# Start addresses in SBUF: every tile that TensorE reads moved to a multiple of 64 bytes

## The chip, the cores and the metric

The kernel runs on one core of a Trainium2 chip. The metric is the time of one execution on the device in microseconds (us), as a median of several executions. A core has five engines: TensorE (PE) multiplies matrices, VectorE (DVE), ScalarE (ACT) and GpSimd (POOL) do elementwise work, and SyncE (SP) issues transfers. A matmul has two inputs, both read from SBUF, the memory of 128 partitions beside the engines: the stationary one (here mostly 128 columns), which is loaded ahead, and the moving one, whose columns (here mostly 512 or 272) then stream through. Each tile of SBUF begins at the same byte offset in every partition; that offset is what this case changes.

## The reference

The input is x (64 sequences of 32 tokens, 512 features). Two layers follow, each added to x:

```
x = x + lora_moe_0(long_convolution(x))      # W_base, 8 experts of rank 16, top 2
x = x + lora_moe_1(paged_attention(x))       # same form, other weights
long_convolution: a kernel of 512 taps per channel from a state space model, masked by length
paged_attention:  q = x Wq (32 heads of 128), k, v = x Wk, x Wv (8 heads), RMS norm and rotation
                  of q and k, 512 cached keys per sequence found by a block table plus 32 own
                  keys, softmax, times the values, times Wo
lora_moe:         x W_base + b + sum over experts of weight * (x A_e) B_e
```

All is float32. To keep its precision on the faster path (type fp32r), the kernel splits a factor into an upper and a lower part (names ending in `hi` and `lo`) and multiplies three times: hi by hi, hi by lo and lo by hi.

## The kernel before, in words

The program is one long sequence of stages, and each engine has its own list of instructions, written out by hand, with semaphores between them. There is no planner.

- `prologue`: turns the cached keys (L378), computes the taps, and convolves (L399).
- `ffn` for layer 0: gate (L625), base product (L666, L667, L671: 192 matmuls of 512 columns in 4 column blocks of 48), first factor of the experts (L648 to L650: 48 matmuls), second factor (L681 to L683: 48 matmuls). Moving are `xh`, `xl`; stationary are the halves of the weights, `pr_hi` and `pr_lo`. For the second factor moving is `f_hw`, stationary `f_lb`.
- `project`: 160 tiles of queries and keys, then 32 tiles of values. A tile is 12 matmuls of 512 columns (L762 hi*hi, L763 hi*lo, L764 lo*hi, four times), with `xh` or `xl` stationary and the weights moving. For queries and keys a tile also takes four transposes on PE (L981, five tiles later) and, on the other engines, squares (ACT L868), the mean (DVE L904), the root (ACT L880), the reciprocal (DVE L908), the normed tile `pr_qn` (DVE L911), the two products with the tables of the rotation (DVE L922, POOL L942, two instructions) and their sum (DVE L918). In four of 16 tiles DVE also makes the lower half of the next weights (L751). PE writes the tiles to four banks of PSUM in turn, and so waits for L911 of four tiles earlier. Values need none of this: ACT copies them out (L893) and SP stores them.
- `attention`: 512 steps, one head of one sequence each. A step has 6 matmuls of 272 columns for the scores (L1209), 4 transposes (L1218) and 4 matmuls with the cached values (L1242); every fourth step adds own values (L1249).
- `output_projection`: 32 units, 8 groups of heads by 4 blocks of 512 tokens. A unit is 48 matmuls of 512 columns: for each of 4 column blocks, 8 of L1529 and L1530 (upper and lower weights by `op_ohi`) and 4 of L1534 (upper weights by `op_olo`). Units alternate between two buffers of the moving operand: units 0, 2, ... read `op_ohi0` and `op_olo0`, units 1, 3, ... read `op_ohi1` and `op_olo1`. The stationary `op_whi` and `op_wlo` change every 4 units.
- `ffn` for layer 1: as for layer 0, with `f1_x_hi` and `f1_x_lo` moving and `f1_w_hi` and `f1_w_lo` stationary.

Tiles are placed one behind the other, each start rounded up to 32 bytes, from the left by `sbuf_tensor` and from the right with `side="right"`; `Early` and `Late` place tiles at offsets counted from `place`, the end of `shared`. The table of constants is 769 numbers wide, 3076 bytes, so `shared` and what stands behind it begin 32 bytes past a multiple of 64.

Of the kernel before, what the change touches and what calls it, by code (L numbers as in the profile page):

```python
# [15 lines left out]
F32 = mybir.dt.float32  # L16
# [7 lines left out]
P = 128  # L24
B, S, L = 64, 32, 512
T = B * S
KB = L // P
NS = 64
HP = S // 2
E, R = 8, 16  # L30
# [7 lines left out]
KC = LK // P  # L38
# [21 lines left out]
C_ROW = C_DESC + E  # L60
C_REV = C_ROW + KB
C_MOD = C_REV + KB
C_ALL = C_MOD + 1


def constants():

    c = np.zeros((P, C_ALL), np.float32)
    c[:, C_ID:C_ID + P] = np.eye(P)
# [13 lines left out]
class Line:  # L83


    def __init__(self, eng, sem):
        self.eng, self.sem, self.n = eng, sem, 0
# [54 lines left out]
def prologue(nc, ps, dram, taps, cst, um, mrow, k_t, y_t, cos, sin, ta, tb, inputs):  # L142
# [9 lines left out]
    with ExitStack() as ctx:  # L152
# [32 lines left out]
        with nc.Block() as block:  # L185
            @block.sync
            def _(e):
                src = bass.AP(tensor=dram["L0_cond_log_dt"].tensor, offset=0, ap=[[0, P], [1, S]])
                e.dma_start(log_dt[:, :], src).then_inc(s_dt, 16)
                e.dma_start(raw[:, 1, :], dram["log_a"]).then_inc(s_dt, 16)  # L190
                e.dma_start(ai[:, :], dram["a_imag"]).then_inc(s_in, 16)
                e.dma_start(cc[:, :, :], dram["c"]).then_inc(s_in, 16)
                e.dma_start(dvec[:, :], dram["L0_cond_D"].rearrange("(o h) -> o h", o=1)).then_inc(s_in, 16)

                def load(n):
                    e.dma_start(k_in[:, n % TB, :], dram["k_cache"][n * P:(n + 1) * P, :]).then_inc(s_ki[n % TB], 16)

                for n in range(TB):
                    load(n)
                k_rows = k_t.rearrange("(t n d) x -> t d n x", n=PPT, d=P)  # L200
                for n in range(KT):
                    e.wait_ge(s_kc, 2 * (n + 1))
                    e.dma_start(k_rows[n:n + 1, :, :, :].rearrange("o d n x -> (o d) n x"),
                                k_out[:, n % TB, :, :, :].rearrange("p n g k -> p n (g k)")).then_inc(s_ko[n % TB], 16)
                    if n + TB < KT:
                        load(n + TB)
                    if n + TB == KT:
                        inputs.load(e, dram, ("w0", "b0", "g0", "a0", "lb0"))
                for q in range(TB):
                    e.wait_ge(s_ko[q], 16 * KT // TB)  # L210
# [106 lines left out]
            def _(e):  # L317
# [39 lines left out]
                for h in range(TOE):  # L357
                    load(h)
# [48 lines left out]
class Inputs:  # L407


    def __init__(self, nc, ctx, sems, tag, at=None):  # L410
        def sb(n, shape):
            if at is None:
                return ctx.enter_context(nc.sbuf_tensor(f"f{tag}_{n}", shape, F32))
            x = nc.alloc_sbuf_tensor_at(f"f{tag}_{n}", shape, F32, offset=self.end)
            self.end += (math.prod(shape[1:]) * 4 + 31) // 32 * 32
            return x

        self.end = at
        self.w = sb("w", [P, KB, L])
        self.a = sb("a", [P, KB, E * R])  # L420
        self.g = sb("g", [P, KB, S])
        self.lb = sb("lb", [E * R, L])
        self.bias = sb("bias", [P, KB])
        self.s_z, self.s_g, self.s_w, self.s_a, self.s_b = (
            sems.enter_context(nc.semaphore(f"f{tag}_{n}")) for n in ("s_z", "s_g", "s_w", "s_a", "s_b"))

# [4 lines left out]
    def load(self, e, dram, names):  # L431

        w_n, b_n, g_n, a_n, lb_n = names
        e.wait_ge(self.s_z, 1)
        e.dma_start(self.g[:, :, 0:E], dram[g_n].rearrange("(k p) e -> p k e", p=P)).then_inc(self.s_g, 16)
        e.dma_start(self.w[:, :, :], dram[w_n].rearrange("(k p) o -> p k o", p=P)).then_inc(self.s_w, 16)
        e.dma_start(self.bias[:, :], dram[b_n]).then_inc(self.s_w, 16)
        e.dma_start(self.a[:, :, :], dram[a_n].rearrange("(k p) r -> p k r", p=P)).then_inc(self.s_a, 16)
        e.dma_start(self.lb[:, :], dram[lb_n]).then_inc(self.s_b, 16)

# [546 lines left out]
        return s_proj, s_stage, s_t, s_qr, stores  # L987


LATE_SMALL = 4 * (KB * (L + E * R + S) + L + KB)  # L990


class Early:
# [3 lines left out]
    def __init__(self, nc, sems, at):  # L997
        def place(n, shape, d=F32):
            size = math.prod(shape[1:]) * 4
            x = nc.alloc_sbuf_tensor_at("at_" + n, shape, d, offset=self.end)  # L1000
            self.end += (size + 31) // 32 * 32
            return x

        self.end = at
        self.v_raw = place("v_raw", [P, 2, KC, HK * D])
        self.leni = place("leni", [P, B], I32)
        self.lenf = place("lenf", [P, B])
        self.pagef = place("pagef", [P, B * KC])
        self.rows = place("rows", [P, B * KC], U32)
        self.page = place("page", [P, B * NPP], I32)  # L1010
        self.idx = place("idx", [P, 2, KC], U32)
        self.mask = place("mask", [P, 2, NKEY])
        self.pr_new = place("pr_new", [P, 2, REP * S])
        self.nm, self.su, self.ri = (place(n, [P, 2 * REP]) for n in ("nm", "su", "ri"))
        place("gap", [P, 168])
        self.q_hi = place("q_hi", [P, 2, HK * P], F32R)
        self.ot = place("ot", [P, 2, HK * P])

        self.chunks = [nc.alloc_sbuf_tensor_at(f"f0_resid{q}", [P, KB, 512], F32, offset=self.end - (1 - q) * 4 * 2 * 2 * HK * P)
                       for q in range(2)]  # L1020
        self.more = nc.alloc_sbuf_tensor_at("pr_more", [P, 2, 512], F32, offset=self.end + 4 * HK * P)
        self.q_lo = place("q_lo", [P, 2, HK * P], F32R)
        self.v_new = place("v_new", [P, 2, 2, REP * D])
        self.k_hi, self.k_lo = (place(n, [P, 2, 2, NKEY], F32R) for n in ("k_hi", "k_lo"))
        place("gap2", [P, 256])
        place("gap4", [P, 2 * LK])
        place("gap3", [P, 32])
        self.s_in, self.s_qhi = (sems.enter_context(nc.semaphore("at_" + n)) for n in ("in", "qhi"))
# [7 lines left out]
class Late:  # L1036
# [4 lines left out]
    def __init__(self, nc, sems, at, keys):  # L1041
        def place(n, shape, offset, d=F32):
            return nc.alloc_sbuf_tensor_at(n, shape, d, offset=offset)

        w, o = REP * L * 4, 512 // S * P * 4
        small = at + 2 * KC * HK * D * 4
        sums = small + (LATE_SMALL + 31) // 32 * 32
        split = sums + KB * T * 4
        self.w_hi, self.w_lo = ([place(f"op_w{h}{q}", [P, REP, L], at + (2 * q + i) * w, F32R) for q in range(2)]
                                for i, h in enumerate(("hi", "lo")))  # L1050
        self.o_hi, self.o_lo = ([place(f"op_o{h}{q}", [P, REP, 512], (keys + i * o, split + i * 2 * 2 * NKEY * 4)[q], F32R)
                                 for q in range(2)] for i, h in enumerate(("hi", "lo")))
        self.att = place("att", [P, KB, T], sums)
        self.x_hi = place("f1_x_hi", [P, KB, T], at, F32R)
        self.inputs = Inputs(nc, None, sems, "1", small)
        self.end = split
        self.s_whi, self.s_wlo, self.s_ohi, self.s_olo = (sems.enter_context(nc.semaphore("op_" + n)) for n in ("whi", "wlo", "ohi", "olo"))
# [482 lines left out]
def build(nc, dram, out_t):  # L1540
# [9 lines left out]
    with ExitStack() as ctx:  # L1550
        ps = ctx.enter_context(nc.psum_tensor("ps", [P, 8, 512], F32))
        cst = ctx.enter_context(nc.sbuf_tensor("constants", [P, C_ALL], F32))

        KT_SIZE, QK_SIZE = 2 * (NPP + 1) * HK * PSIZE, 2 * HK * P
        shared = ctx.enter_context(nc.sbuf_tensor("shared", [P, KT_SIZE + QK_SIZE], F32))
        y_t = shared[:, 0:KB * T].rearrange("p (k t) -> p k t", k=KB)
        angles = shared[:, KB * T:KB * T + NT * D].rearrange("p (two t h) -> p two t h", two=2, t=NT)
# [5 lines left out]
        place = nc.sbuf_base  # L1563
        with ExitStack() as sems:
            sb = lambda c, n, s, d=F32, side=None: c.enter_context(nc.sbuf_tensor(n, s, d, side=side))
# [80 lines left out]
```

## Time and profile before

| | us |
|---|---|
| median of 3 runs | 2441.7 (2440.74 to 2443.94) |
| the profiled execution, whole | 2454.87 |
| its span, first to last instruction | 2453.0 |
| PE busy in it | 2400.6 |
| DVE busy in it | 1878.4 |
| ACT busy in it | 1310.2 |
| POOL busy in it | 719.9 |

The profile is of one execution. Matmuls overlap, and the end of each is modelled, so the time that a matmul costs in a stream is the distance between two starts. The granted clock of TensorE is given as a share of full speed, which is 2.4 GHz; its mean here is 0.997.

### The profile page before, as it was taken

The page shows a single profiled execution, that of the slowest core. Times are in us where ns is not written, and L with a number is a line of the kernel's source. Part 1 is how long each engine was busy: PE and PEld are TensorE (multiplying, and loading weights), DVE is VectorE, ACT ScalarE, POOL GpSimd, SP SyncE. Part 2 cuts the span into 40 slices and gives each one's busy share as a digit, 9 for nine tenths or more (in the row PEclk, how much of TensorE's full clock was granted, in tenths as well). Part 3 has the DMA queues.
Part 4 walks back from the last instruction along what each step waited for, and adds up shares of the span by engine and source line. Part 5 has one row for each costly group of instructions (what it writes and reads, how often), then busy time and mean ns, then how long its engine had stood idle before and what let it go on. Part 6 is the DMA issues. An engine that isn't in the chain of part 4 may idle for free. (4 is left out here: it accounts for less than half of the span.)

```text
span 2453.0 us, 53992 instructions
## 1 busy us (share of the span) xinstructions
PE 2400.6 (98%) x16104; PEld 2167.1 (88%) x16104; DVE 1878.4 (77%) x3317; ACT 1310.2 (53%) x3758; POOL 719.9 (29%) x712
## 2 busy tenths in 40 slices
PE   5999999999999999999999999999999999999999
PEld 4888777777777999999999999999999998888877
DVE  7559999999961887788778877788778876666653
ACT  2335555555543677677767776676667761111120
POOL 1206666666641122222222222222222213131100
PEclk9999999999999999999999999999999999999999
DMA  8732333333347688888888888888788879666622
GB/s 312 258 120 87 94 98 95 95 115 94 98 125 245 222 295 276 294 298 291 281 285 303 295 284 282 293 297 295 273 295 295 295 268 283 219 209 207 204 69 103
DMA packets 434117, 542.36 MB, mean 221 GB/s; under 512 B 36980, under 2 KB 350100, under 8 KB 429460
## 3 DMA queue, kind: packets, MB, share of 16 engines
q1 hardware_dynamic: 390724, 394.24, 48.7%
q0 software_dynamic: 36864, 134.23, 16.2%
q10 hardware_dynamic: 6480, 13.26, 1.5%
q8 instruction: 28, 0.46, 0.1%
q14 instruction: 21, 0.17, 0.0%
HBM read 440.59 MB, written 101.01 MB: 221 GB/s over the span
## 5 line engine op out<-in xcount | busy, mean ns | idle before, releaser
L1296 DVE CUSTOM_DVE_ANT_0 at_sm<-ps,at_mask 128x544 f32<-128x544 f32 x512 | 369.3, 721 | 256.2 <-PE ps L1209 247.7
L1242 PE MATMUL ps<-at_pt,at_v_raw 128*128 128x128 f32 x4096 | 540.9, 275 | 1.7 <-issue 1.7
L1242 PEld LDWEIGHTS ps<-at_pt,at_v_raw 128*128 128x128 f32 x4096 | 497.6, 192 | 1.9 <-issue 1.9
L1359 ACT ACTIVATE at_pt<-ps 128x512 f32<-128x512 f32 x512 | 303.9, 594 | 299.4 <-PE ps L1218 194.9
L942 POOL TENSOR_TENSOR pr_m<-pr_qn,tb 128x256 f32<-128x256 f32 x320 | 331.6, 1056 | 307.0 <-DVE pr_qn L911 291.8
L1372 ACT ACTIVATE at_pr<-at_sm,at_nm 128x544 f32<-128x544 f32 x512 | 383.1, 748 | 59.1 <-DVE at_nm L1296 54.9
L1289 DVE TENSOR_TENSOR at_k_lo<-shared,at_k_hi 128x1088 fp32r<-128x1088 f32 x256 | 325.9, 1273 | 0.0
L762 PE MATMUL ps<-pr_hi,xh 128*128 (+1 forms) x768 | 317.7, 414 | 6.1 <-DVE pr_qn L911 5.0
L1167 POOL DMA_INDIRECT at_v_raw<-v_cache,at_idx x256 | 276.9, 1082 | 113.9 <-issue 62.0
L1218 PE MATMUL ps<-constants,at_pr 128*128 128x128 f32 x2048 | 306.5, 272 | 0.0
L764 PE MATMUL ps<-pr_hi,xl 128*128 (+1 forms) x768 | 303.3, 395 | 0.0
L763 PE MATMUL ps<-pr_lo,xh 128*128 (+1 forms) x768 | 303.2, 395 | 0.0
L868 ACT ACTIVATE pr_sq<-ps 128x128 f32<-128x128 f32 x640 | 168.0, 277 | 229.7 <-DVE f_a L904 224.4
L1173 POOL COPY at_idx<-at_rows 128x4 uint32 (+1 forms) x64 | 11.8, 184 | 868.4 <-PE ps L1249 801.7
L1209 PE MATMUL ps<-at_k_hi,at_q_hi 128*128 128x272 f32 x1024 | 255.5, 330 | 3.1 <-issue 1.2
L1218 PEld LDWEIGHTS ps<-constants,at_pr 128*128 128x128 f32 x2048 | 243.5, 140 | 0.0
L1209 PE MATMUL ps<-at_k_hi,at_q_lo 128*128 128x272 f32 x1024 | 211.9, 288 | 0.0
L1209 PE MATMUL ps<-at_k_lo,at_q_hi 128*128 128x272 f32 x1024 | 211.2, 287 | 0.0
L1477 ACT ACTIVATE op_ohi<-o_raw 128x2048 fp32r<-128x2048 f32 x31 | 59.6, 1922 | 273.5 <-PE ps L1534 243.1
L1530 PE MATMUL ps<-op_ohi,op_wlo 128*128 128x512 f32 x512 | 201.2, 393 | 0.0
L1529 PE MATMUL ps<-op_ohi,op_whi 128*128 128x512 f32 x512 | 200.9, 392 | 0.0
L922 DVE TENSOR_TENSOR pr_m<-pr_qn,ta 128x512 f32<-128x512 f32 x160 | 195.9, 1224 | 0.0
(239 smaller groups left out, 4299.3 us busy)
## 6 DMA issues: line engine op xcount, KB each, us to landing
shared<-k_t SPq DMA_DIRECT2D x1024, 128.0 KB
qk_t<-pr_stage SPq DMA_DIRECT2D x160, 256.0 KB, 2.3
shared<-qk_t SPq DMA_DIRECT2D x64, 512.0 KB, 7.3
o_t<-at_ot SPq DMA_DIRECT2D x64, 512.0 KB
shared<-ri_d SPq DMA_DIRECT2D x32, 1024.0 KB, 8.3
o_raw<-o_t SPq DMA_DIRECT2D x32, 1024.0 KB, 6.1
f_w<-wqkv SPq DMA_DIRECT2D x12, 1024.0 KB, 5.9
s_k_in<-k_cache SPq DMA_DIRECT2D x16, 512.0 KB, 8.0
```

Of the source, the lines that this page charges most:

```text
L762: e.matmul(out, xh[:, k, cols], hi, start=(k == 0), stop=False)
L763: e.matmul(out, xh[:, k, cols], lo, start=False, stop=False)
L764: last = e.matmul(out, xl[:, k, cols], hi, start=False, stop=(k == KB - 1))
L942: ins = e.tensor_tensor(heads(m2[:, q, :])[:, :, a], heads(qn[:, q, :])[:, :, b], table(tb, i, j - 3, a), ALU.mult)
L1167: e.indirect_dma_start(out=v_raw[:, q, c, :], out_offset=None, in_=dram["v_cache"], in_offset=bass.IndirectOffsetOnAxis(ap=idx[:, q, c:c + ...
L1209: last = e.matmul(ps[:, 2 * r + h, 0:W], a[:, q, mine], b[:, w, g % 2, h * W:(h + 1) * W], start=first, stop=end)
L1218: last = e.transpose(ps_w(jj % 2)[:, c * P:(c + 1) * P], pr[:, w, k, c * P:(c + 1) * P], ident)
L1242: e.matmul(sums(w, k), v_raw[:, q, c, g * D:(g + 1) * D], pt[:, jj % 4, c * P:(c + 1) * P], start=(k == 0 and c == 0), stop=False, skip_gr ...
L1289: e.tensor_tensor(two(k_lo), raw, two(k_hi).bitcast(F32), ALU.subtract).then_inc(s_lo, 1)
L1296: e.tensor_tensor_reduce(out=halves(sm[:, r, :]), in0=ps[:, 2 * r:2 * r + 2, 0:W], in1=halves(mask[:, q, :]), scale=-SC, scalar=3e38, op0= ...
L1359: e.activation(pt[:, jj % 4, :], ps_w(jj % 2), ACT.Copy).then_inc(s_pt, 1)
L1372: e.activation(pr[:, w, k, :], sm[:, r, :], ACT.Exp, bias=nm[:, at], scale=-1.0, accum_out=su[:, at]).then_inc(s_e, 1)
```

## The change

The table of constants is padded from 769 to 784 columns. The tiles of the two biases are 16 wide in place of 4 (4 are used). A gap of 32 bytes comes behind `at_idx`. A gap of 32 bytes comes at the right end, so that the tiles from the right lie 32 bytes lower. `sums` in `Late` needs no rounding any more. No instruction is added, removed or moved on any engine: the lists read the same, apart from numbers of lines and of buffers. A transfer of the constants carries 3136 bytes for each partition, 3076 before.

```diff
-C_ALL = C_MOD + 1
+ALIGN = 16
+C_ALL = (C_MOD + ALIGN) // ALIGN * ALIGN
...
-        self.bias = sb("bias", [P, KB])
+        self.bias = sb("bias", [P, ALIGN])[:, 0:KB]
...
-        e.dma_start(self.bias[:, :], dram[b_n]).then_inc(self.s_w, 16)
+        e.dma_start(self.bias, dram[b_n]).then_inc(self.s_w, 16)
...
-LATE_SMALL = 4 * (KB * (L + E * R + S) + L + KB)
+LATE_SMALL = 4 * (KB * (L + E * R + S) + L + ALIGN)
...
         self.idx = place("idx", [P, 2, KC], U32)
+        place("gap0", [P, ALIGN - 2 * KC])
...
-        sums = small + (LATE_SMALL + 31) // 32 * 32
+        sums = small + LATE_SMALL
...
         KT_SIZE, QK_SIZE = 2 * (NPP + 1) * HK * PSIZE, 2 * HK * P
+        ctx.enter_context(nc.sbuf_tensor("right_gap", [P, nc.sbuf_top // 4 % ALIGN], F32, side="right"))
         shared = ctx.enter_context(nc.sbuf_tensor("shared", [P, KT_SIZE + QK_SIZE], F32))
```

Start addresses, in bytes from the start of a partition, as the two programs place the tiles, and what is left of each after division by 64 and by 128. Slices that matmuls read begin at multiples of 64 bytes from a tile's start (most at multiples of 512), so the remainder by 64 is that of the tile.

| tile | role on PE | before | by 64, 128 | after | by 64, 128 |
|---|---|---|---|---|---|
| `constants` (identity) | moving, transposes | 16512 | 0, 0 | 16512 | 0, 0 |
| `shared` | stationary in L639, moving in L625 of layer 0 | 19616 | 32, 32 | 19648 | 0, 64 |
| `op_ohi0` | moving | 37024 | 32, 32 | 37056 | 0, 64 |
| `op_olo0` | moving | 45216 | 32, 32 | 45248 | 0, 64 |
| `op_whi0`, `at_v_raw` | stationary | 62624 | 32, 32 | 62656 | 0, 64 |
| `f1_x_hi` | moving | 62624 | 32, 32 | 62656 | 0, 64 |
| `at_q_hi`, `pr_hi` | stationary; moving in L762 | 108224 | 0, 64 | 108288 | 0, 0 |
| `at_v_new` | stationary | 132800 | 0, 64 | 132864 | 0, 0 |
| `op_ohi1`, `at_k_hi` | moving | 140992 | 0, 64 | 141056 | 0, 0 |
| `op_olo1`, `at_k_lo` | moving | 149696 | 0, 64 | 149760 | 0, 0 |
| `f1_w_hi` | stationary | 157376 | 0, 64 | 157440 | 0, 0 |
| `at_pr` | stationary, transposes | 168000 | 0, 64 | 168064 | 0, 0 |
| `f1_x_lo` | moving | 177856 | 0, 64 | 177920 | 0, 0 |
| `at_pt` | moving | 185408 | 0, 64 | 185472 | 0, 0 |
| `at_pt_new` | moving | 193600 | 0, 64 | 193664 | 0, 0 |
| `f1_lb_hi`, `f1_hw_hi` | stationary, moving | 217728, 221824 | 0, 0 | 217792, 221888 | 0, 64 |
| `xl` | moving in layer 0, stationary in `project` | 163808 | 32, 96 | 163776 | 0, 64 |
| `xh` | the same | 196576 | 32, 96 | 196544 | 0, 64 |

## Rows read from the trace of the kernel before

**Rows 1.** The page: granted clock in 40 slices, in tenths of full speed.

```profile
PEclk9999999999999999999999999999999999999999
```

**Rows 2.** Waits of PE: line, waited for, us in total, times, longest.

```profile
PE ps L378 <- DMA s_k_in<-k_cache: 21.5, 9, 12.0
...
PE ps L762 <- DVE pr_qn L911: 5.0, 26, 0.2
```

**Rows 3.** Stretches: us, busy (instructions) of PE, PEld, DVE, ACT, POOL, PEclk, DMA.

```profile
795.00:2015.50 1220.50, 1215.39 (x10432) 1205.51 (x10431) 969.67 (x1988) 856.88 (x1925) 281.73 (x311) 1.00 0.85 287
2015.50:2369.50 354.00, 354.00 (x1539) 288.04 (x1537) 221.86 (x187) 60.18 (x32) 78.15 (x57) 1.00 0.63 205
```

**Rows 4.** Timeline of PE: first matmul of units 16, 17, 18 (`output_projection`).

```profile
2192.58 0.40 PE L1529 MATMUL ps<-op_ohi,op_whi 128*128 128x512 f32 x1
...
2203.49 0.40 PE L1529 MATMUL ps<-op_ohi,op_whi 128*128 128x512 f32 x1
...
2214.70 0.40 PE L1529 MATMUL ps<-op_ohi,op_whi 128*128 128x512 f32 x1
```

**Rows 5.** Groups on PE, 2194 to 2203 us (unit 16): busy, mean ns.

```profile
L1530 PE MATMUL ps<-op_ohi,op_wlo 128*128 128x512 f32 x14 | 5.5, 389 | 0.0
```

**Rows 6.** Groups by line on PE, 2204 to 2214 us (in unit 17).

```profile
L1530 PE MATMUL ps<-op_ohi,op_wlo 128*128 128x512 f32 x16 | 6.3, 396 | 0.0
```

**Rows 7.** Groups by line on PE, 740 to 790 us (tiles of values).

```profile
L762 PE MATMUL ps<-pr_hi,xh 128*128 128x512 f32 x72 | 28.5, 396 | 0.0
```

**Rows 8.** Groups by line and shape on PE, whole span.

```profile
L1242 PE MATMUL ps<-at_pt,at_v_raw 128*128 128x128 f32 x4096 | 540.9, 275 | 1.7 <-issue 1.7
L1218 PE MATMUL ps<-constants,at_pr 128*128 128x128 f32 x2048 | 306.5, 272 | 0.0
...
L1209 PE MATMUL ps<-at_k_lo,at_q_hi 128*128 128x272 f32 x1024 | 211.2, 287 | 0.0
...
L1249 PE MATMUL ps<-at_pt_new,at_v_new 128*128 128x128 f32 x1024 | 135.4, 275 | 0.4 <-ACT at_pt_new L1364 0.4
...
L666 PE MATMUL ps<-xh,pr_hi 128*128 128x512 f32 x64 | 25.6, 400 | 0.0
L666 PE MATMUL ps<-f_x_hi,f_w_hi 128*128 128x512 f32 x64 | 25.5, 398 | 0.0
...
L671 PE MATMUL ps<-xh,pr_lo 128*128 128x512 f32 x64 | 17.5, 395 | 0.0
...
L671 PE MATMUL ps<-f_x_hi,f_w_lo 128*128 128x512 f32 x64 | 17.4, 394 | 0.0
...
L639 PE MATMUL ps<-constants,shared 128*128 128x128 f32 x32 | 4.8, 272 | 0.0
```

**Rows 9.** Timeline of PE in layer 1, second factor of the experts.

```profile
2411.92 0.39 PE L681 MATMUL ps<-f_hw_hi,f_lb_hi 128*128 128x512 f32 x1
2412.14 0.39 PE L682 MATMUL ps<-f_hw_hi,f_lb_lo 128*128 128x512 f32 x1
...
2413.05 0.40 PE L683 MATMUL ps<-f_hw_lo,f_lb_hi 128*128 128x512 f32 x1
```

**Rows 10.** Timeline of DVE in `project`, two tiles.

```profile
437.52 0.69 DVE L911 TENSOR_TENSOR pr_qn<-ps,f_a 128x512 f32<-128x512 f32 x1
...
440.70 0.69 DVE L911 TENSOR_TENSOR pr_qn<-ps,f_a 128x512 f32<-128x512 f32 x1
```

**Rows 11.** L911 alone in six chunks of `project`: us, busy (instructions).

```profile
328.57:648.65 320.08, 66.41 (x96) 1.00 0.34 98
```

**Rows 12.** Timeline of PE in `project`: the transposes of two tiles.

```profile
301.50 0.60 PE L981 MATMUL ps<-constants,pr_qr 128*128 128x128 f32 x4
...
304.73 0.60 PE L981 MATMUL ps<-constants,pr_qr 128*128 128x128 f32 x4
```

**Rows 13.** Groups by line and shape on DVE.

```profile
L507 DVE TENSOR_TENSOR f_x_lo<-att,f_x_hi 128x512 fp32r<-128x512 f32 x16 | 10.0, 685 | 1.0 <-ACT f_x_hi L586 1.0
L507 DVE TENSOR_TENSOR xl<-shared,xh 128x512 fp32r<-128x512 f32 x16 | 10.0, 684 | 1.0 <-ACT xh L586 1.0
```

## The prediction

> **What bounds the kernel now.** I began with the page's row of the granted clock: full speed (2.4 GHz) in all 40 slices [rows 1], so cycles and time can be exchanged at 2.4 GHz. PE is busy for 2400.6 of 2453.0 us. The waits of PE come next: the largest, 21.5 us, is for transfers in the prologue, and only 5.0 us are for DVE in `project` [rows 2]. The stretches say the same of the two large stages behind it: PE is busy for 1215.39 of 1220.50 us in attention and for all of 354.00 in the output projection [rows 3]. A nanosecond saved for each matmul there is saved at the end. `project` is different. PE looks full, but L911 on DVE starts every 3.18 us [rows 10], PE's transposes every 3.23 us [rows 12], and the mean over 96 tiles is 320.08 / 96 = 3.334 us [rows 11]. The rest of the mean is L751 on DVE, which falls on four of 16 tiles. DVE, with POOL's half of the rotation, has the longer list over a chunk, and PE waits for it a little at a time.
>
> **Does a start address matter to a matmul?** The trace holds an experiment. Units 16 and 17 of the output projection run the same 48 matmuls with the same weights and differ in the moving buffer alone. They take 10.91 and 11.21 us [rows 4], so 227.3 and 233.5 ns for each matmul. Twelve to 16 matmuls of a line show it as a mean of 389 against 395 or 396 ns [rows 5, 6]. 512 columns at 2.4 GHz are 213.3 ns; 226.7 is 544 cycles and 233.3 is 560, so the difference is 16 cycles, or 6.67 ns. The slow buffer is the one at a multiple of 64 (140992), the fast one begins 32 bytes past (37024). The stationary side is 32 past in both. So it isn't alignment itself but the difference between the two operands: equal remainders by 64 are fast, unequal ones slow. The other stages agree. Values (moving 0, stationary 32) are slow, 396 ns [rows 7]. Both base products (moving 32 for two thirds or all, stationary 0) lie at 394 to 400 [rows 8]. The second factor of layer 1 (0 and 0) settles at (2413.05 - 2411.92) / 5 = 226 ns [rows 9], so two zeros are as fast as two 32s. The change makes all remainders by 64 zero.
>
> It leaves differences of 64 by 128: values go to moving 0, stationary 64, and units 1, 3, ... too. Before has such a case: in the scores, the second half of each key tile begins 1088 bytes further, at 0 by 128, with the queries at 64. L1209 takes 287 ns for 272 columns [rows 8], 173.7 over its 113.3; fast matmuls of 512 are 175.7 over their 213.3 and slow ones 182 over. Were every second one slow, the mean would be near 292. So 64 against 128 costs nothing, and I take 64 as what counts.
>
> The Trainium skill speaks against all of this. SBUF — State Buffer (section on the two separate sides) says that contention on the engine side comes only from the port pair of VectorE and GpSimd and that PE never waits on anyone; TensorE: Matmul & The Clock Gate (Part 2, on the phases) gives PE two independent read ports and about 216 ns between matmuls of 512 columns. By these the change gives 0 us. The trace disagrees where it can be compared: 227.3 and 233.5 ns for the same work.
>
> **The change part by part.**
>
> *Output projection.* A pair of units takes 22.12 us [rows 4]. At 226.7 ns for all 96 it would be 21.76. 16 pairs: 16 x 0.36 = 5.7 us. PE has no wait here, so all of it counts.
>
> *Tiles of values.* Of 32 tiles the first eight run beside the end of the queries and keys, which DVE sets; the other 24 are a plain stream: 288 x 6.67 ns = 1.9 us. The next stage begins with PE's last tile, so it counts.
>
> *Base products.* 192 matmuls a layer, at about (400 + 395) / 2 = 397.5 ns in layer 0 and (398 + 394) / 2 = 396 in layer 1 [rows 8], 8.5 and 7 above the 389 of a fast one. Not all of it goes: a stream that begins anew needs some matmuls to settle, as unit 16's loss shows (10.91 us against 48 x 226.7 ns = 10.88), and the first behind transposes is longer in any case. I take 6 and 5 ns: 192 x 11 ns = 2.1 us. The two factors of the experts (96 matmuls each, half of them already equal) add 0.3.
>
> *Queries and keys.* 1920 matmuls would gain 2 to 6 ns each, 4 to 12 us, were PE the bound. It isn't: DVE's list stays at 3.334 us a tile [rows 11], and PE's saving becomes a longer wait of L762 on L911. I count 0.1 us, for the first tile. Could DVE itself change? L507 takes 684 ns with three operands 32 past and 685 with the inputs and output mixed [rows 13]: no. For POOL there is no pair of rows.
>
> *Attention.* The scores keep their relation, and so do the own values. The cached values (L1242) have moving 0 and stationary 32 now and equal remainders after. Their mean is 275 ns, and that of L1249, equal already, is 275 too; transposes are 272 with equal (L1218) and unequal remainders (L639) [rows 8]. In plain float32 the difference between the operands does nothing: 0 us. Bounds: if the new position gave L1242 the 272 of a transpose, 4096 x 3 ns = 12.3 us would go; if it cost the 6.67 ns of fp32r, 27.3 us would come.
>
> *Prologue, transfers, padding.* 60 bytes more of constants for each partition, in one transfer: at most 0.1 us. What PE waits for there, L378 on `s_k_in` [rows 2], begins at a multiple of 64 both times. 0, with 1 us either way.
>
> The sum is 5.7 + 1.9 + 2.4 + 0.1 = 10.1 us: the profiled execution of 2454.87 us would take 2444.8. It ran 13.2 us above the median; the difference carries over, so 2441.7 - 10.1 = 2431.6 us.
>
> **The rivals.**
>
> *A: larger granules.* If 128 bytes count, values, units 1, 3, ... and the base products end at a difference of 64 and stay slow; units 0, 2, ... stay fast. Nothing moves: 2441.5. For it: no stream of 512 columns in the trace shows a difference of 64. Against: the 287 ns of L1209. By the two pages of the Trainium skill named above, too, the time would stay where it is.
>
> *B: half of it.* Streams keep falling out of the fast rhythm. Then half of each term goes: about 2436.8. Against: unit 16 settles and stays.
>
> *C: cached values gain.* L1242 gets to 272 ns: 10.1 + 12.3 = 22.4, 2419.3. Only the bound speaks for it; L1249 speaks against.
>
> *D: slower.* The price falls on attention. L1242's two operands start to meet as those of fp32r do, at 6.67 ns for each of 4096: 27.3 - 10.1 = +17.2 us, 2458.9. From 2.5 ns each on (10.1 us / 4096) this outweighs the gain. For it: `at_pt` and `at_v_raw` come to a difference of 64, which this line never had, and PE is full in this stage, so nothing hides it. Against: L1249 with a difference of 0 and L1242 with 32 both take 275.
>
> **How the numbers follow.** Forecast 0.60, A 0.15, B 0.12, C 0.05, D 0.08. This kernel's runs differ by 0.13%, so 0.2% (4.9 us) is about what can be told from no change: faster means below 2436.8. Faster: 0.60 + 0.05 and half of B, 0.71. Same: A and half of B, 0.21. Slower: D, 0.08. The forecast's own range is 2429 to 2434.5. With A and B the range is 2428.5 to 2443; C and D and a little of the rest, 0.17, lie outside.
>
> **What would show it.** Right: units of the output projection all at 10.9 us; the means of L1529, L1530 and L1534 at 389; values at 389 or 390; tiles of queries and keys still 3.33 us apart, with more waiting of L762 on L911; L1242 still at 275. Wrong: alternate units still at 11.2 (A); a mean between (B); attention longer or shorter than 1220 us (C, D); `project` below 3.33 us a tile, which would mean that DVE or POOL feel addresses as well.

## The result, and the profile after

| | us |
|---|---|
| before, median of 20 runs | 2443.81 (2440.74 to 2448.12) |
| after, median of 20 runs | 2439.95 (2437.27 to 2442.83) |
| ratio after to before | 0.9982, 95% interval 0.9976 to 0.9988 |
| the profiled execution of after, whole and span | 2441.24, 2439.4 |

The change makes the kernel faster, by 4.4 us by the ratio (2.9 to 5.9; the two medians are 3.9 us apart), where 10.1 us were forecast. The direction is right and the size is less than half. Of the forecast's three large terms one came in half, one in two thirds, and one hardly at all.

The lines of `kernel.py` stand one or two further down in the kernel after: L763 there is L762 before, L1531 is L1529. In the output projection the timeline of PE again shows the first matmul of units 16, 17 and 18, of the kernel after (columns: start us, us, engine, line):

```profile
2180.71 0.40 PE L1531 MATMUL ps<-op_ohi,op_whi 128*128 128x512 f32 x1
...
2191.64 0.40 PE L1531 MATMUL ps<-op_ohi,op_whi 128*128 128x512 f32 x1
...
2202.64 0.40 PE L1531 MATMUL ps<-op_ohi,op_whi 128*128 128x512 f32 x1
```

The units take 10.93 and 11.00 us, before 10.91 and 11.21 [rows 4]. The odd unit gained 0.21 us and stays slower than the even one: 229.2 ns a matmul, neither the 226.7 that I forecast nor the 233.5 of before. The groups of PE by line for the kernel after, in the tiles of values (740 to 785 us; columns as in [rows 7]), say the same:

```profile
L765 PE MATMUL ps<-pr_hi,xl 128*128 128x512 f32 x67 | 26.4, 394 | 0.0
L764 PE MATMUL ps<-pr_lo,xh 128*128 128x512 f32 x66 | 25.9, 392 | 0.0
L763 PE MATMUL ps<-pr_hi,xh 128*128 128x512 f32 x66 | 25.6, 388 | 0.0
```

Their mean is 391 ns, between 389 and 396. The base products hardly moved. The whole span by line and shape, kernel after (of before: [rows 8]):

```profile
L667 PE MATMUL ps<-xh,pr_hi 128*128 128x512 f32 x64 | 25.5, 398 | 0.0
...
L667 PE MATMUL ps<-f_x_hi,f_w_hi 128*128 128x512 f32 x64 | 25.3, 395 | 0.0
...
L672 PE MATMUL ps<-xh,pr_lo 128*128 128x512 f32 x64 | 17.5, 395 | 0.0
L672 PE MATMUL ps<-f_x_hi,f_w_lo 128*128 128x512 f32 x64 | 17.5, 395 | 0.0
```

L672 stands at 395 in both layers, where 389 would be fast, though all the remainders by 64 are equal now. Queries and keys did nearly as forecast. L912 (L911 before) alone, in six chunks of `project` of the kernel after, and PE's wait for it (line, us in total, times, longest):

```profile
331.00:651.00 320.00, 66.40 (x96) 1.00 0.32 98
```

```profile
PE ps L763 <- DVE pr_qn L912: 7.0, 27, 0.3
```

These are 96 tiles in 320.0 us as before [rows 11], and PE waits 7.0 us, before 5.0 [rows 2]. This list counts only what is idle after the modelled end of a matmul; the starts show more. Over 110 tiles in the middle of the stage the 12 matmuls of a tile take 31 ns less from the first start to the last, and the gap to the next tile's first is 27 ns longer (707 against 680). So DVE's list sets this stage, and most of PE's saving became a wait. Attention is told below, since its length in a profile has nothing to do with the change.

### The profile page after: what moved, and what is told of

It reads as the page before. It is cut to its first block and busy times, and to the rows that moved or that the text cites. A ratio compares the mean times of both kernels' runs of the same rounds, so it can differ in the third digit from the quotient of the medians.

```text
span 2439.4 us, 53992 instructions
## 1 busy us (share of the span) xinstructions
PE 2383.5 (98%) x16104; PEld 2164.6 (89%) x16104; DVE 1888.7 (77%) x3317; ACT 1320.7 (54%) x3758; POOL 718.7 (29%) x712
## 5 line engine op out<-in xcount | busy, mean ns | idle before, releaser
L763 PE MATMUL ps<-pr_hi,xh 128*128 (+1 forms) x768 | 316.3, 412 | 8.9 <-DVE pr_qn L912 7.0
L1288 DVE CAST at_k_hi<-shared 128x1088 fp32r<-128x1088 f32 x256 | 194.3, 759 | 8.0 <-DMA shared<-qk_t 7.4
L1531 PE MATMUL ps<-op_ohi,op_whi 128*128 128x512 f32 x512 | 200.5, 392 | 0.0
```

What stands on the lines that cost most here:

```text
L763: e.matmul(out, xh[:, k, cols], hi, start=(k == 0), stop=False)
```

## The experiments

The stages of every profile of the kernel, in us, each from the start of its first matmul on PE to the start of the next stage's first; the last one ends with DVE's last addition. From profile to profile of one kernel most repeat to 0.1 us, queries and keys to 0.3, and the output projection of `equal256` by 0.6, because units 1 and 2 took 10.98 and 11.40 us in one of its profiles and 10.88 in the other. Left out are the prologue, the gates and attention, which vary from one execution to the next whatever the kernel, and the first eight tiles of values.

| kernel | base and experts, layer 0 | queries, keys | later 24 tiles of values | output projection | base and experts, layer 1 | sum |
|---|---|---|---|---|---|---|
| before | 68.92 | 528.69 | 67.30 | 357.01 | 69.35 | 1091.3 |
| again_before | 68.92 | 528.40 | 67.29 | 357.00 | 69.35 | 1091.0 |
| after | 68.81 | 527.93 | 66.03 | 354.03 | 69.26 | 1086.1 |
| again_after | 68.81 | 527.92 | 66.05 | 353.99 | 69.26 | 1086.0 |
| after_beside | 68.81 | 528.02 | 66.03 | 354.03 | 69.26 | 1086.2 |
| left_only | 68.76 | 527.93 | 67.30 | 354.00 | 69.27 | 1087.3 |
| right_only | 67.33 | 528.19 | 65.41 | 357.00 | 69.39 | 1087.3 |
| equal256 | 67.33 | 527.79 | 65.42 | 351.92 | 68.29 | 1080.8 |
| equal256_beside | 67.32 | 528.05 | 65.41 | 351.30 | 68.29 | 1080.4 |
| right128 | 68.66 | 528.07 | 67.04 | 351.92 | 68.28 | 1084.0 |

So the change saves 5 us in these stages (4.8 to 5.2 by the profiles chosen), in line with the 4.4 measured, and nothing of it is lost elsewhere. The other half of the forecast was never gained.

### Both kernels again

No edit, a second profile of each.

> The kernel before, unchanged, profiled a second time. In its first profile a step of attention took 2.374 us on average and the stage 1220.5 us; the kernel after took 2.348 and 1209.6, though its matmuls have the same spacing there. Theory 1: that longer attention belongs to the one execution that was profiled (it ran 11 us above the median of the unprofiled ones), so the stage is 1210 us here. Rival: the start addresses lengthen it, so it is 1220 us again. Output projection 357.0 us and plain tiles of values 2.800 us in either case.

> The kernel after, unchanged, profiled a second time. The output projection should again take 354.0 us and a plain tile of values 2.750 us if the start addresses set them. The convolution (49.7 us against 47.8 before) and the gate of layer 0 (6.5 against 5.2, with the granted clock at half) were longer in its first profile: by theory 1 that is chance and goes away or varies here, by the rival it belongs to the addresses and returns.

Measured: one time each, 2462.17 us before, 2457.43 after, and 2457.88 for the kernel before once more beside them, without a profile. All three lie 14 us or more above the medians of the result. It isn't a slower chip: the same chip gave 2443.20 us for the kernel before in the next session. In the two profiled executions the excess is about that of attention (1228.2 and 1229.3 us, where most profiles have some 1210). Theory 1 was wrong for it, and it is not the addresses either. The stretch of attention in the kernel before (first fence) and in the kernel after in its second profile (second fence), with the columns of [rows 3]:

```profile
794.96:2023.13 1228.17, 1221.07 (x10433) 1207.41 (x10432) 969.42 (x1988) 857.62 (x1925) 283.70 (x311) 1.00 0.84 285
```

```profile
792.16:2021.47 1229.31, 1222.74 (x10434) 1208.37 (x10432) 969.71 (x1988) 857.23 (x1925) 282.85 (x311) 1.00 0.84 285
```

Both kernels have it long here, and the first profile of after has it short:

```profile
795.52:2005.16 1209.64, 1204.87 (x10434) 1202.27 (x10432) 980.18 (x1988) 866.95 (x1925) 281.73 (x311) 1.00 0.86 289
```

Attention has two rhythms, 1208 to 1212 us in seven of the ten profiles and 1220 to 1229 us in three. By the starts of the transposes seven of eight steps are alike in both (within 0.03 us), and the eighth takes 2.29 to 2.34 us in the long rhythm, 2.07 or 2.08 in the short one. ACT then waits for something that the profile doesn't name ("remote"): in the waits of the second profile of before, 900 to 1900 us (us in total, times, longest), the rows are

```profile
ACT at_pt L1359 <- PE ps L1218: 154.2, 216, 3.0
ACT at_pt L1359 <- remote: 89.6, 53, 2.5
```

and in the first profile of after, which is short, there is only the first of them:

```profile
ACT at_pt L1361 <- PE ps L1220: 240.7, 419, 0.7
```

The long rhythm comes with either kernel, so a comparison of two single profiles can show 11 us that the change did not make. What sets it I did not find out; it stays open. The convolution (48.8 and 47.8 us here against 47.8 and 49.7 in the first two) and the gate of layer 0 (5.2 in both) vary from execution to execution, as theory 1 had it.

### Streams at chosen addresses

Not the kernel, but 40 streams like this one, back to back; what differs is the start of the two slices (`m` and `s` in bytes; the fence gives the pattern, the program has each stream written out):

```diff
+for i in range(64):
+    last = e.matmul(ps[:, bank, 0:512], st_r[:, s // 4 + i % 8 * P:...], mv_r[:, m // 4 + i % 4 * 512:...],
+                    start=(i == 0), stop=(i == 63))
```

> A kernel that computes nothing of the reference: 40 streams of 64 matmuls, each stream with its own start of the moving operand (0 to 480 bytes by 32) and of the stationary one, nothing else running on PE's operands. Theory M64 (only the remainder by 64 of the difference counts): 226.7 ns for differences of 0, 64, 128, ..., 233.3 for 32, 96, ... Theory M256 (the difference by 256 counts, with its sign, as read from the kernel after: 0 gives 226.7, moving 64 ahead 229.2, moving 192 ahead 233, and 32 and 224 ahead 233.3): a curve of 8 values that repeats from 256 on. Rival: both at 0 is fast because of alignment itself, and equal remainders of 32 or 64 are slower than 226.7. For 272 columns and for plain float32 of 128 columns: no difference by any theory.

Measured, by groups of lines of its profile, stationary at 0 (columns: busy us, mean ns; moving at 160, 32, 192, 96, 128, 224, 64 and 0 in this order):

```profile
L81 PE MATMUL ps<-mv_r,st_r 128*128 128x512 f32 x64 | 15.2, 396 | 0.0
...
L65 PE MATMUL ps<-mv_r,st_r 128*128 128x512 f32 x64 | 15.1, 395 | 0.0
L85 PE MATMUL ps<-mv_r,st_r 128*128 128x512 f32 x64 | 15.1, 396 | 0.0
...
L73 PE MATMUL ps<-mv_r,st_r 128*128 128x512 f32 x64 | 15.1, 395 | 0.0
L77 PE MATMUL ps<-mv_r,st_r 128*128 128x512 f32 x64 | 15.1, 395 | 0.0
...
L89 PE MATMUL ps<-mv_r,st_r 128*128 128x512 f32 x64 | 15.1, 395 | 0.0
...
L69 PE MATMUL ps<-mv_r,st_r 128*128 128x512 f32 x64 | 14.8, 391 | 0.0
...
L61 PE MATMUL ps<-mv_r,st_r 128*128 128x512 f32 x64 | 14.7, 389 | 0.0
```

The distance from start to start, as a mean over the last 47 distances of each stream, with the stationary slice at 0:

| moving ahead of stationary, by 256 | 0 | 32 | 64 | 96 | 128 | 160 | 192 | 224 |
|---|---|---|---|---|---|---|---|---|
| ns | 226.7 | 233.3 | 229.0 | 233.4 | 233.2 | 234.4 | 233.3 | 233.3 |
| cycles over 512, at 2.4 GHz | 32 | 48 | 37.5 | 48 | 48 | 50.5 | 48 | 48 |

Starts from 256 to 480 repeat the curve to 0.05 ns. Both at 32 and both at 64 give 226.7 like both at 0, so it is the difference that helps and not the alignment of either; the sign matters too (stationary 64 ahead, which is 192, is 233.3). Other steps: 16 bytes give 231.7, 48 give 230.0, 4 give 236.9. M256 holds, M64 and the rival fall. One point departs: stationary 128 ahead gave 232.4 where moving 128 ahead gave 233.2. The other forms feel little. Matmuls of 272 columns, moving at 0, 64 and 192 (mean ns; 126.6, 126.7 and 123.3 from start to start):

```profile
L177 PE MATMUL ps<-mv_r,st_r 128*128 128x272 f32 x64 | 8.3, 291 | 0.0
L185 PE MATMUL ps<-mv_r,st_r 128*128 128x272 f32 x64 | 8.2, 289 | 0.0
...
L193 PE MATMUL ps<-mv_r,st_r 128*128 128x272 f32 x64 | 8.1, 286 | 0.0
```

At 32 they take 125.7. This is the point that undoes my argument: a stream of 272 columns is as quick at 32, where 512 columns are slow, as at 0. A matmul of 128 columns in plain float32 leaves two records, and these stand 111.7 ns apart at all five starts.

Set beside the two programs' addresses this accounts for the means above. In the output projection odd units went from 32 to 64 (233.3 to 229.2), even ones stayed at 0. Values went from 224 to 64. The base product of layer 0 has the same tiles in exchanged roles, so it went from 32 to 192, both 233.3. In layer 1 `f1_x_hi`, which two thirds of the matmuls read, went from 224 to 192, and `f1_x_lo` stayed at 0. So the gain in both base products was next to nothing.

### One part of the change at a time

`right_only` is before with nothing but the gap at the right end:

```diff
+        ctx.enter_context(nc.sbuf_tensor("right_gap", [P, 8], F32, side="right"))
```

> One part of the change alone: the tiles from the right (xh, xl, um, mrow, later o_raw and w_raw) lie 32 bytes lower, all else as before. xh and xl come to 192 by 256, where pr_hi and pr_lo already are, so in the plain tiles of values and in the base product of layer 0 the difference of the two operands is 0 by 256. Theory M256 (the curve measured in the streams): values 226.7 ns a matmul, 2.720 us a tile instead of 2.800 (24 tiles, 1.9 us), base product and first factor of layer 0 about 1.2 us less, output projection unchanged at 357.0: 3.1 us faster than before, more than the whole change gives in these stages (1.5 us). Rival, the whole shift is needed (both operands at multiples of 64 count by themselves): values 233, nothing gained.

Measured 2442.61 against 2443.20 us, ratio 0.9994 (0.9985 to 1.0003): the times can't be told from no change. By the table the stages save 3.6 to 4.0 us, at the end of that interval (3.7 us), so here the stages speak and the times do not. The stages are as M256 has them: values 65.41, base 67.33, both below the kernel after, though `shared` and `op_whi0` are still 32 past a multiple of 64. The rival of the expectation isn't settled by this run alone, since `xh` and `pr_hi` both lie at multiples of 64 here; the streams with both at 32 settle it. Values in its profile, 740 to 785 us:

```profile
L763 PE MATMUL ps<-pr_lo,xh 128*128 128x512 f32 x67 | 26.1, 389 | 0.0
L764 PE MATMUL ps<-pr_hi,xl 128*128 128x512 f32 x67 | 26.1, 389 | 0.0
```

`left_only` is after without that gap:

```diff
-        ctx.enter_context(nc.sbuf_tensor("right_gap", [P, nc.sbuf_top // 4 % ALIGN], F32, side="right"))
```

> The whole change but for the gap at the right end: xh and xl stay at 224 by 256, their partners pr_hi and pr_lo are at 0. M256: difference of 32 or 224, so values 2.800 us a tile and the base product of layer 0 68.8 to 69.0 us as before, output projection 354.0 us as in the kernel after: about 3.1 us faster than before (0.9987). Rival, the right side is what matters and the left does nothing: output projection 357.0.

Measured 2439.33 against 2443.97 us, ratio 0.9977 (0.9967 to 0.9986), 3.7 to 4.0 us by the stages. Output projection 354.00, values back at 67.30, base at 68.76: as expected. The left side carries the 3.0 us of the output projection, and, against the profile of before, 0.8 in queries and keys; `right_only` has 0.5 there, and the second profile of before alone differs by 0.3 from the first, so that this stage can't be shared out between the sides. Alone the two sides save 3.8 and 3.9 us, together only 5: the right gap brings `xh` and `xl` to 192, where `pr_hi` and `pr_lo` are in the kernel before, and the padding on the left moves these two on to 0.

### All differences at zero

`equal256` moves the two biases into spare columns of the constants and shortens a gap, which brings both operands of every fp32r stream of 512 columns to the same remainder, nearly all to 192 by 256 (the lines that hand the table of constants on are left out):

```diff
-        self.bias = sb("bias", [P, ALIGN])[:, 0:KB]
+        at_bias = C_MOD + 1 + KB * int(tag)
+        self.bias = cst[:, at_bias:at_bias + KB]
...
-LATE_SMALL = 4 * (KB * (L + E * R + S) + L + ALIGN)
+LATE_SMALL = 4 * (KB * (L + E * R + S) + L)
...
-        place("gap", [P, 168])
+        place("gap", [P, 152])
```

> The kernel after with the two biases moved into spare columns of the table of constants and the gap in Early 64 bytes shorter, so that pr_hi, pr_lo, op_ohi1, op_olo1, f1_w_hi, f1_w_lo and f1_x_lo lie at 192 by 256 like op_whi, op_wlo, f1_x_hi, xh and xl: the difference of the two operands is 0 by 256 in every stream of 512 columns. M256: all units of the output projection 10.88 us (stage 351 us against 357.0 before and 354.0 after), values 2.720 us a tile, base products 66.7 to 67.8 us instead of 68.8, about 9.9 us faster than before (0.996). M64: as fast as the kernel after, 0.998, since all remainders by 64 were zero there already.

Measured 2434.55 against 2443.20 us, ratio 0.9964 (0.9951 to 0.9978), 8.7 us between the medians. The stages of this and the next profile of it save 10.2 to 10.9 us. From the fourth on the units of the output projection take 10.88 us each, odd and even alike, and their groups of lines, 2186 to 2196 us, are all fast:

```profile
L1532 PE MATMUL ps<-op_ohi,op_whi 128*128 128x512 f32 x16 | 6.2, 389 | 0.0
L1533 PE MATMUL ps<-op_ohi,op_wlo 128*128 128x512 f32 x15 | 5.8, 389 | 0.0
L1537 PE MATMUL ps<-op_olo,op_whi 128*128 128x512 f32 x15 | 4.0, 389 | 0.0
```

It was then timed in one session with the kernel after, on the same chip:

> The kernel after, unchanged, timed beside the next one. Stages as in its two profiles: output projection 354.0 us, later tiles of values 66.0 us, base products 68.8 and 69.3. By the stages it is 5.0 us faster than before (0.998).

> The kernel with all differences 0 by 256, timed again beside the kernel after. By the stages of the profiles 10 us faster than before and 5 us faster than the kernel after: output projection 351.9 us against 354.0, later tiles of values 65.4 against 66.0, base products 67.3 and 68.3 against 68.8 and 69.3. If the two come out equal in time, the gain in the stages is lost elsewhere.

Measured: after 2439.37 us, ratio 0.9978 (0.9969 to 0.9987); `equal256` 2434.44 us, 0.9955 (0.9942 to 0.9969), before 2443.97. It is faster than both kernels: its slowest execution took 2436.33 us, the fastest of the kernel after beside it 2436.94. The medians are 4.9 us apart, the stages 5.2 to 5.8. Against before its medians stand 8.7 and 9.5 us lower, which is about the gain that I forecast for the change (10.1).

`right128` takes `equal256` and moves the right side 128 bytes lower:

```diff
-"right_gap", [P, nc.sbuf_top // 4 % ALIGN]
+"right_gap", [P, nc.sbuf_top // 4 % ALIGN + 32]
```

> As equal256, but the tiles from the right 128 bytes lower still: xh and xl at 64 by 256, their partners at 192, every tile that TensorE reads still a multiple of 64, and these pairs equal even by 128. M256: values back at 2.799 us a tile and the base product of layer 0 at 68.9 us, output projection fast as in equal256, about 6.8 us faster than before. A modulus of 64 or 128: the same as equal256.

Measured 2435.86 us, ratio 0.9968 (0.9955 to 0.9982), 7.0 to 7.3 us by the stages. Values (67.04) and base product of layer 0 (68.66) are slow again, with all these tiles at multiples of 64 and the pairs equal by 128. Values, 740 to 785 us:

```profile
L765 PE MATMUL ps<-pr_lo,xh 128*128 128x512 f32 x65 | 25.6, 395 | 0.0
L764 PE MATMUL ps<-pr_hi,xh 128*128 128x512 f32 x65 | 25.6, 395 | 0.0
```

The times of this and `equal256` overlap; the stages do not. A modulus of 64 or 128 falls.

### Could the scores gain as well?

Streams as above with 272 columns, and then the sequence of a step of attention (6 scores, 4 transposes, 8 values) with the keys at eight starts. A matmul of values, in plain float32, leaves two records. The kernel's own step has 4 with 8 records (4096 for 512 steps [rows 8]), so the step here holds twice as many.

> A kernel that computes nothing of the reference: 8 streams of 64 matmuls of 272 columns with the moving operand at 0, 32, ..., 224 bytes and the stationary one at 0, then 8 streams of 16 steps with the sequence of attention (6 scores, 4 transposes, 8 values, 18 matmuls a step), with the keys at 0 to 224. The first streams of 272 gave 126.6, 125.7, 126.7, 126.7 and 123.3 ns at 0, 32, 64, 128 and 192. If that holds beside transposes and values, a step is up to 6 x 1.7 = 10 ns shorter with keys at 192 than at 0, worth 5 us over 512 steps; if the matmuls between scores set the rhythm anew, all eight steps are within 3 ns.

Measured, from one step's first transpose to the next, as a mean over 11 steps: 2973.4 ns with the keys at 0, then 2990.2, 2984.8, 2976.5, 2979.8, 2976.9, 2986.7 and 2973.6 at 32, 64, ..., 224. The quick stream at 192 (123.4 ns here too) is worth nothing beside transposes and values; its step is 13 ns longer than at 0. The expectation missed on both sides: the spread is 17 ns, not 3 and not a gain of 10. Nothing here speaks for moving the keys. The test is for the heads whose keys start at 0; in the kernel every second head's start 128 bytes further.

## Why the prediction was wrong

The step that failed is this sentence on scores of 272 columns: "So 64 against 128 costs nothing, and I take 64 as what counts." By it the sum counted as fast what ended at a difference of 64 by 256 (odd units of the output projection, values) or of 192 (base products).

- *That the difference of the two starts matters, not alignment.* Right. It was read from two units that differ in one buffer, and the streams with both operands at 32 or at 64 show it directly. The two pages of the Trainium skill, SBUF — State Buffer (section on the two separate sides) and TensorE: Matmul & The Clock Gate (Part 2), would have the change give 0 us. The runs, all of this in fp32r, do not agree: one and the same stream takes 226.7 ns or 233.3 by the two starts.
- *The modulus.* Wrong. It is 256, and the curve has a sign. In the trace of before, differences by 256 were only 0, 32 and 224 in the streams of 512 columns, so nothing there could tell 64 from 256. I filled the gap with L1209 and took its 287 ns as proof that 64 is fast. By 256 its differences are 0 and 64 for one head and 128 and 192 for the next, but that form is as quick at 32 too (125.7 ns against 126.6 at 0), so it could prove nothing: I had not asked whether it would have shown the slow case. Rival A held the better question and got 0.15.
- *Output projection*, forecast 5.7 us, measured 3.0. Odd units went to 229.2 ns, not 226.7. With the differences at zero it is 5.1 and 5.7 in two profiles.
- *Values*, forecast 1.9, measured 1.3; 1.9 with the differences at zero.
- *Base products and experts*, forecast 2.4, measured 0.2. The pairs went from one slow difference to another (in layer 1 two thirds of them, the rest were at 0 all along). With zero 1.6 and 1.1, together 2.7.
- *Queries and keys*, forecast 0.1, measured 0.4 to 0.8, of which two profiles of one kernel differ by 0.3. That DVE holds the stage was right, the mean per tile hardly moved (3.334 and 3.330 us over 96 normed tiles).
- *Attention*, forecast 0. Its matmuls kept their spacing (cached values 275 ns long and 111.7 ns apart in both kernels). C and D fell.
- *Carrying over to the median.* The profiled execution of before stood 13 us above the median shown. Some 11 of them were attention's long rhythm; it did no harm to the sum, but the stages, not two spans, had to be compared. The median of three from which I subtracted, 2441.7, also lay 2.1 us below that of 20 (2443.81): of the 8.4 us between the forecast 2431.6 and the measured 2439.95, 2.1 are this and the rest is gain that did not come.

The gain came out near that of B (half of the sum, 5 us, against 4.4 measured), but that is chance and not B's mechanism: streams do not fall in and out of the fast rhythm, each keeps its own. Why a difference of the starts costs cycles, and why just these, no run here shows.

## What to carry to other kernels

A stream of matmuls of 512 columns of fp32r, each with its own load of 128 columns, runs about 3% quicker (226.7 against 233.3 ns) when the moving and the stationary slice begin at the same remainder by 256 bytes; a multiple of 64 alone can leave it as slow as before. Count what that is worth only in stages where PE sets the time, and check a form in isolation before using it as a witness: one that shows no difference may be blind to it. Where a trace holds only two or three values of a quantity, a rule read from it is open between them, and a run with all values took 0.59 ms here.

## What the runs showed of the hardware that I had not expected

- The curve of the table above: of eight differences by 32 bytes 0 is the quickest (32 cycles more than the 512 columns), 64 costs 5.5 cycles on top of that, the others 16 to 18.5, and 4 bytes cost 24 (236.9 ns).
- For 272 columns the order is another: 123.3 ns at 160 and 123.4 at 192, 125.3 at 224, 125.7 at 32, and 126.6 or 126.7 at 0, 64, 96 and 128.
- Plain float32 of 128 columns does not feel the difference (111.7 ns between records at 0, 32, 64, 128 and 192, two records for each matmul).
- Attention of one and the same kernel runs in one of two rhythms, 1208 to 1212 us or 1220 to 1229 us, with one of eight steps 0.2 to 0.3 us longer.
